# One words load per four and a new order of the first stores in a conditioned residual kernel

## The reference

```
x = x + einsum('bct,bcd->bdt', x, W0[cond0])             # W0: 200 tables of 128x128, one index word per batch
x = x + einsum('bct,bcd->bdt', x, W1[cond1]) + bias[cond1]  # W1: 8 tables of 128x128, bias: 8x128
```

## Time and profile before

| | |
|---|---|
| Time, median of 3 runs | 347.63 us (347.43 to 348.22) |
| The profiled execution's own time | 348.84 us |
| Its span, first to last instruction | 347.1 us |
| Granted TensorE clock, mean | 0.961 |
| Busy share of the span: PE, PEld, DVE, ACT, POOL | 77%, 37%, 36%, 28%, 19% |
| DMA | 140.80 MB, mean 406 GB/s; HBM read 76.03 MB, written 67.11 MB |
| Chain that ended last | DMA 56%, SP's queue 27%, issue 9%, PE 5% |

### The profile page before, as it was taken

How to read it: one execution, slowest core, us unless ns; L and a number is a source line. 1 busy time by engine, 2 the same in 40 slices (tenths; PEclk the granted TensorE clock), 3 DMA queues, 4 the chain that set the end, 5 groups by cost and what they waited for, 6 DMA issues and landing times.

```text
span 347.1 us, 5157 instructions
## 1 busy us (share of the span) xinstructions
PE 266.8 (77%) x774; PEld 129.5 (37%) x774; DVE 126.3 (36%) x202; ACT 96.9 (28%) x135; POOL 65.3 (19%) x249
## 2 busy tenths in 40 slices
PE   1799991986798896979877779777679877778980
PEld 1344450442344442434433334433334433333430
DVE  3254541333334242433433344333334333334440
ACT  1133350221333133332232232422242222323230
POOL 2400222112221112221122212122221212221000
PEclk9999997899989898998999999999999999999996
DMA  7999969999999999999999999999999999999994
GB/s 306 410 409 393 378 248 351 424 418 397 417 431 415 433 423 427 417 416 427 432 425 427 427 423 432 421 436 423 419 431 425 432 430 426 423 421 440 419 405 171
DMA packets 24058, 140.80 MB, mean 406 GB/s; under 512 B 2673, under 2 KB 14322, under 8 KB 15474
## 3 DMA queue, kind: packets, MB, share of 16 engines
q1 hardware_dynamic: 23760, 140.20, 97.9%
q10 hardware_dynamic: 290, 0.53, 0.4%
HBM read 76.03 MB, written 67.11 MB: 412 GB/s over the span
## 4 chain that ended last, share of the span: by engine, by line
DMA 56%; SPq 27%; issue 9%; PE 5%; ACT 0%
DMA out<-xy 47%; SPq L127 10%; DMA xy<-x 9%; SPq L122 7%; PE y_ps L306 5%; SPq L128 4%; SPq L142 3%; SPq L145 2%; ACT xy L402 0%; PE m_ps L287 0%; SPq L159 0%; SPq L148 0%; SPq L153 0%; SPq L163 0%; SPq L154 0%
## 5 line engine op out<-in xcount | busy, mean ns | idle before, releaser
L306 PE MATMUL y_ps<-xy,m_sb 128*128 128x512 f32 x512 | 245.5, 616 | 61.3 <-DMA xy<-x 60.3
L306 PEld LDWEIGHTS y_ps<-xy,m_sb 128*128 128x128 f32 x512 | 92.9, 196 | 164.9 <-issue 164.9
L402 ACT ACTIVATE xy<-y_ps,j_pick 128x512 f32<-128x512 f32 x128 | 87.9, 687 | 233.1 <-PE y_ps L306 233.1
L378 DVE TENSOR_SCALAR xy<-y_ps,j_pick 128x512 f32<-128x512 f32 x128 | 96.1, 751 | 156.5 <-PE y_ps L306 156.5
L238 POOL COPY w_pick<-w_home 128x128 f32 x112 | 32.8, 293 | 245.4 <-issue 245.4
L287 PEld LDWEIGHTS m_ps<-j_pick,w_pick 128*128 128x128 f32 x224 | 35.4, 199 | 28.7 <-issue 28.7
L370 DVE TENSOR_TENSOR m_sb<-m_ps,j_pick 128x256 f32<-128x256 f32 x64 | 27.1, 424 | 45.2 <-PE m_ps L287 44.6
L287 PE MATMUL m_ps<-j_pick,w_pick 128*128 128x128 f32 x224 | 35.1, 281 | 0.0
L240 POOL COPY j_pick<-j_all 128x129 f32 x112 | 33.0, 295 | 0.1
L402 ACT ACT_TABLE_LOAD x7 | 9.0, 1283 | 7.9 <-POOL j_pick L252 7.8
L287 PE MATMUL m_ps<-j_pick,w_home 128*128 128x128 f32 x32 | 5.5, 297 | 6.7 <-DMA w_home<-w_t 6.7
(11 more groups left out here) (16 smaller groups left out, 2.8 us busy)
## 6 DMA issues: line engine op xcount, KB each, us to landing
xy<-x SPq DMA_DIRECT2D x30, 2048.0 KB, 15.1
out<-xy SPq DMA_DIRECT2D x29, 2048.0 KB, 13.4
w_home<-w_t SPq DMA_DIRECT2D x128, 64.0 KB
out<-xy SPq DMA_DIRECT2D x5, 1024.0 KB, 6.8
xy<-x SPq DMA_DIRECT2D x3, 1024.0 KB, 7.8
xy<-x SPq DMA_DIRECT2D x4, 256.0 KB, 12.6
j_all<-w_bias SPq DMA_DIRECT2D x1, 516.0 KB, 3.7
out<-xy SPq DMA_DIRECT2D x2, 256.0 KB, 5.1
```

The costliest lines, as they stand in the source:

```text
L306: nc.tensor.matmul(y_ps[:, b % YB, h, :], m_sb[:, s, k, :], xy[:, s, k, half(h)], start=True, stop=True).then_inc(y_ready, 1)
L378: nc.vector.tensor_scalar(xy[:, s, k, half(0)], y_ps[:, b % YB, 0, :], j_pick[:, s, k, D:D + 1], None, ALU.add).then_inc(left_out[b % YB], 1)
L402: nc.scalar.activation(xy[:, s, k, half(1)], y_ps[:, b % YB, 1, :], ACT.Identity, bias=j_pick[:, s, k, D:D + 1]).then_inc(right_out[b % YB ...
```

## The change

It does three things. First, `words_of` is called once for a four (eight words) and no longer once for a pair (four words); in round 0 it is four words in place of two. Second, the range of the words is given at the load, with the run-time check left out there, and the two `s_assert_within` of each w0 load are gone. Third, the order from L186 on is written out anew: each pair of w0 of (1,0) and (1,1) is put between stores, and the w0 of (1,2) and (1,3) come one step later than before, after the x load of (1,1) and of (1,2). The loop starts at another step (q from 3 to 6), and its order is the same as before.

```diff
             def words_of(words):
                 return nc.values_load_multi_w_load_instructions(
-                    words, engines=(mybir.EngineType.SP,),
-                    skip_runtime_bounds_check_because="each word is checked against its own range below")[1]
+                    words, engines=(mybir.EngineType.SP,), min_val=0, max_val=N0 - 1,
+                    skip_runtime_bounds_check_because="the reference indexes a table of N0 rows with each cond word, "
+                                                      "and each word of need is 0 or 1")[1]
 
             def load_one(b, s, i, needed):
                 sp.dma_start(w0_home[:, bass.ds(b, 1), :].rearrange("k b c -> k (b c)"),
-                             w0_t[bass.ds(nc.s_assert_within(i, 0, N0 - 1), 1), :, :].rearrange("n k c -> (n k) c"),
+                             w0_t[bass.ds(i, 1), :, :].rearrange("n k c -> (n k) c"),
                              cond=needed).then_inc(w0_loaded[s], 16)
 
-            def load_w0_first(s):
-                words = words_of(cond_words[0:1, 0, s * PAIR:(s + 1) * PAIR])
-                for k in range(PAIR):
-                    load_one(s * PAIR + k, s, words[k], None)
-
-            def load_w0(r, s):
-
-                sp.wait_ge(w0_loaded[s], r * (PAIR * 16))
+            def load_w0_first(q):
+                words = words_of(cond_words[0:1, 0, q * QB:(q + 1) * QB])
+                for k in range(QB):
+                    load_one(q * QB + k, q * QUAD + k // PAIR, words[k], None)
+
+            def load_w0(r, s, pairs=1):
+
+                for n in range(s, s + pairs):
+                    sp.wait_ge(w0_loaded[n], r * (PAIR * 16))
                 b = r * ROUND_B + s * PAIR
-                words = words_of(load_words[0:1, bass.ds(b, PAIR), :].rearrange("o b f -> o (b f)"))
-                for k in range(PAIR):
-                    load_one(b + k, s, words[2 * k], nc.s_assert_within(words[2 * k + 1], 0, 1))
+                words = words_of(load_words[0:1, bass.ds(b, pairs * PAIR), :].rearrange("o b f -> o (b f)"))
+                for k in range(pairs * PAIR):
+                    load_one(b + k, s + k // PAIR, words[2 * k], words[2 * k + 1])
...
             def load_w0_of(r, q):
-                for s in range(q * QUAD, (q + 1) * QUAD):
-                    load_w0(r, s)
+                load_w0(r, q * QUAD, QUAD)
...
             for q in range(QUADS):
-                for s in range(q * QUAD, (q + 1) * QUAD):
-                    load_w0_first(s)
+                load_w0_first(q)
                 if q < QUADS - 1:
                     load_quad(0, q + 1)
 
 
             sp.wait_ge(home_ready, 4)
-            load_w0_of(1, 0)
-            for s in range(QUAD + 1):
-                store_pair(0, s)
+            load_w0(1, 0)
+            store_pair(0, 0)
+            load_w0(1, 1)
+            store_pair(0, 1)
+            load_w0(1, 2)
+            store_pair(0, 2)
             load_quad_again(1, 0)
-            load_w0_of(1, 1)
-            store_pair(0, QUAD + 1)
+            store_pair(0, 3)
+            load_w0(1, 3)
+            store_quad(0, 2)
+            load_quad_again(1, 1)
+            load_w0_of(1, 2)
+            store_quad(0, 3)
+            load_quad_again(1, 2)
+            load_w0_of(1, 3)
             with sp.Fori(1, ROUNDS - 1) as r:
-                for q in range(1, QUADS + 1):
-                    now = (r, q) if q < QUADS else (r + 1, 0)
-                    after = (r, q + 1) if q + 1 < QUADS else (r + 1, q + 1 - QUADS)
+                for q in range(QUADS - 1, 2 * QUADS - 1):
+                    now = (r + q // QUADS, q % QUADS)
+                    after = (r + (q + 1) // QUADS, (q + 1) % QUADS)
                     load_w0_of(*after)
-                    store_quad(*((r, q - AHEAD) if q >= AHEAD else (r - 1, q - AHEAD + QUADS)))
+                    store_quad(r + (q - AHEAD) // QUADS, (q - AHEAD) % QUADS)
                     load_quad_again(*now)
 
-            for q in range(1, QUADS):
-                if q < QUADS - 1:
-                    load_w0_of(ROUNDS - 1, q + 1)
-                store_quad(*((ROUNDS - 1, q - AHEAD) if q >= AHEAD else (ROUNDS - 2, q - AHEAD + QUADS)))
-                if q < QUADS - 1:
-                    load_quad_again(ROUNDS - 1, q)
-
+            store_quad(ROUNDS - 1, 0)
             sp.wait_ge(stored[QUADS - 1], stored_once(ROUNDS - 1, QUADS - 1))
```

More of the change, by code:

```diff
@@ L41, in conditioned_residual_kernel @@
     BY_PAIR = 2
-    assert PAIRS % RING == 0 and HALF <= 512 and RING % MB == 0 and ROUND_B % YB == 0
+    assert QUADS == 4 and QUAD == 2 and PAIRS % RING == 0 and HALF <= 512 and RING % MB == 0 and ROUND_B % YB == 0
     with ExitStack() as ctx:
```

## The result

The changed kernel takes 343.61 us in the median of 4 runs (343.02 to 344.06), beside 347.84 for the kernel before in 4 runs. The ratio is 0.988, with a 95% interval of 0.9861 to 0.9899: 4.2 us or 1.2% faster. A second measurement, with more runs, gave 0.9869 (0.9845 to 0.9893). The forecast was 344.3 us in a range of 343.2 to 346.2. Direction, hole and place were right; the gain is larger by 0.9 us, and one part of the reasoning did not hold, as the experiments show.

A forecast was written before the change was run, and what follows sets the result against it. The kernel was taken as transfer-bound: the sum of its transfers plus stretches with idle DMA engines. The median of 347.63 us less 3.3 us for the closed hole gave 344.3 us, all else adding nothing; range 343.2 to 346.2.

The forecast's parts named there:

- hole: 44.0 to 48.5 us: DMA share 0.26, 76 GB/s, engines starved because SP issues the store of (0,2) late.
- The price of the hole: 44.0 to 48.5 us: 3.3 us by DMA share against the steady 1.01; 3.7 by rates, kept for the range.
- the cost of a turn from writing to reading: Rival: w0 bursts between pair stores add turns, 0.8 us each; two leave 1.7 us won, 345.9 us; chance 0.12.
- Part 1: SP's w0 loads: fewer words loads, no range instructions; saves 2.7 us per four in steady state, worth nothing there.
- list of signs: Trace signs of right or wrong: slice six over 400 GB/s, store (0,2) near 38.8 us, span 3.3 us shorter, among others.
- Nothing won: Rival: the hole only moves, the queue running dry somewhere before 64 us; 347.5 us; chance 0.07.
- margin of 4 us: Eight w0 loads end at 58.4 to 59.8 us, while store (0,3) and x of (1,2) are queued until 64.
- The rule weighed in Part 1: Time saved at the issuing sequencer is usually small relative to the DMA; by it the whole change gives 347.6 us.
- Part 3: New order, walked through the front: store (0,2) issued at 38.8 us, x of (1,1) near 45; closes the hole.
- The front gained nothing: Judges a rival: front also rises from 410 to 424 GB/s over 23 us, 0.8 us more, 343.5; chance 0.08.
- new turns: 27 to 44 us, write/read turns: two at 0.8 us (345.9, chance 0.12) or six, 4.8 us (349.1, chance 0.03).

The follow-up runs named there:

- second pair of profiles: Both kernels run once more, unchanged: 348.06 us for the kernel before, 343.41 us for the changed one.
- order alone: The changed kernel's order from L186 on, with the words loads and range instructions of the kernel before: 346.32 us, ratio 0.9961.
- words alone: The changed kernel with the block from L186 to L206 as before (old order, new words loads): 344.29 us, ratio 0.9891.
- cover kernels: The changed kernel with the store of (0,2) held until pair 6, or pair 7, is written: 345.34 us (0.9925) and 348.9 us (1.0028).
- steady words: The kernel before up to x of (1,2), written out, with the new `load_w0` in the loop alone: 346.98 us, ratio 0.9968.
- fill with the old words: The order alone kernel with the w0 of (1,2) and (1,3) moved ahead of x of (1,1) and (1,2): 344.79 us, ratio 0.991.
- kernel held to pair 6: The changed kernel with the store of (0,2) held back until pair 6 is written: 345.34 us, ratio 0.9925.

## Why the prediction was right, and where it was wrong

**The hole, its place and cause: right.** The store of (0,2) was late by its place in SP's order; it left at 38.9 us as foreseen, and holding it back brings the loss back.

**The price: under-sized, by a term that was left out.** "The price of the hole" had 3.3 us and took the stretch behind it as undisturbed, on the ground of its share of 1.01. By rates it is 3.7 us for the hole (76 to 427 GB/s over 4.5 us), 1.4 for the slow stretch behind it, less 0.3 for 34 to 44 us, so 4.8 of the 5.9 us between the first two spans. The second pair of profiles gives 3.8 (68 to 438 GB/s), 1.1 (388 to 419) and less 0.4 (387 to 372), so 4.5 of 4.6 us. The medians are 4.2 and 4.6 us apart. Both errors go the same way; together they were small enough to leave the time inside the range. The row was in hand: 52 to 54 us at 262 GB/s and share 0.99. I gave it to a rival as the cost of a turn from writing to reading, and it was a part of the loss that the change removes (404 GB/s in that window after it). A share says whether the DMA engines are occupied, a rate says what they move.

**Part 1: SP's saving over-sized, and its worth misread.** 2.7 us per four were forecast, by range checks that all go and a words load of 0.7 us. The list of signs had "no L128 or L142 instruction on SP" and the waits doubled. 1.6 us came, since 112 checks stayed and the words load takes 1.15 us. That this is worth nothing in steady state agrees with all runs (424 to 426 GB/s from 80 to 300 us). That it is worth nothing in the front either, the argument against the rival *Nothing won* ("with the old SP pace the new order alone still puts store (0,2) at 38.8"), is where the reasoning failed. The sentence is true of that store (39.2 us in order alone), and the next place broke: eight w0 loads at the old pace end where the queue's work ends, the store of (1,0) leaves at 65.3 us, and the x loads behind it run slow. That rival had named the mechanism, 13.8 us "up to the very end of the queue's work at 64", and gave it 0.07. Order alone gives 1.5 us, words alone 3.5, both 4.2. So the margin of 4 us that the forecast saw at this place was made by SP's faster pace, and since that came to 1.6 us per four and not 2.7, it was 2.5 us.

The rule weighed in Part 1 (the Trainium skill, "DMA: Bandwidth & Descriptors", "Issuing engines are not separate DMA queues", where it is said of DMAs initiated on several engines at once) would have given 347.6 us. The runs agree with it in the loop; in the front, where words alone bring 3.5 us by nothing but issue time, they do not.

**Part 3, the walk through the front: right where it could be checked**, within 0.5 us for the store of (0,2) and x of (1,1), and 1 us for the store of (0,3). The store of (1,0) came at 61.5, not at 58.4 to 59.8. One thing was not foreseen: SP reached the store of pair 0 at 20.38 us, not by 16, for the most part since one of its w0 loads was held at issue for 3.2 us (below). The front kept its 412 GB/s, so it cost nothing that shows.

**The rivals.** The front gained nothing (410 and 412 GB/s from 3 to 26 us). What the new turns could have cost from 27 to 44 us is 0.3 us lost and 0.3 won, not 1.6 or 4.8.

## What to carry to other kernels

Where transfers bound a kernel, list the big issues of the issuing queue beside the time at which their data is ready; one that leaves later than its data, with the queue about to run empty, is worth its delay, and everything that the sequencer does between two landings has to fit in what is queued. A cheaper issue and a better order are two ways to the same cover, so their gains don't add up, and a reorder has to be checked at the next place with little cover too. Small loads belong where the sequencer waits for a landing anyway; and a stretch is to be read by its rate as well as its share.

## What the hardware showed unexpectedly

**x loads that run slow at a full share.** Where the store of (0,2) was late, 48.5 to 63 us, in which x of (1,1) runs, had 367 to 388 GB/s with the share near 1.00: in the kernel before, in both cover kernels, in steady words and in words alone, so also without a hole ahead. With an early store it had 404 to 428, but 393 where the store was early and x of (1,1) itself late (fill with the old words, 47.67 us). In order alone it is the x loads behind the late store of (1,0) that run slow. The x load of (1,0) shows it in the changed kernel too (372 GB/s from 34 to 44 us). In the trace's packets the loss is one of time per packet: in the kernel before, the 16 KB packets that start from 53 to 54 us, where x of (1,1) begins, took 1.16 us in the mean, beside 0.61 in most of the run. What slows them is open; nothing was tried that tells one cause from another.

**Issues are held when much is queued.** A w0 load takes SP 0.34 us in the median. In the changed kernel, where the front's x and w0 loads are issued at a quicker pace, the one issued at 14.6 us took 3.19 us (the maximum of the L129 row above), and the store at 61.5 us took 1.27, behind eight w0 loads. In the kernel held to pair 6 the store of (1,0) took 2.86 us:

```profile
L162 SPq DMA_DIRECT2D out<-xy x1: 2860/2860/2860, 63.1 to 63.1; - x1
```

In the kernel before no w0 load took over 0.38 us, and one pair store 0.87. So it looks as if SP could run only so far ahead of its queue; no run tests that, and the depth at which it is held was not measured.

**A words load under traffic.** The same instruction took 0.30 to 1.97 us in one kernel. The four of the front, four words each, took 0.30 to 0.52; those behind them, mostly of eight words, 1.15 in the median.
